# Eight buffers for the last weights, GpSimd's norm written as an addition, scale products on ScalarE, and one operation for mask and maximum, in a two-layer gated kernel

## The chip, the core and the metric

The kernel runs on one core of a Trainium2 chip. The metric is the device time of one execution in microseconds. The engines are named as the profile names them: PE (TensorE, matmuls), PEld (its weight loads), DVE (VectorE), ACT (ScalarE), POOL (GpSimd), and SP (SyncE), which here issues nearly all DMAs.

## What is computed

Two layers on x of shape (8, 256, 512), each an "attention" and a feed-forward network, both added through a gate:

```python
x = x + tanh(g_xattn[0]) * conv_attention(ctx, ctx, layernorm(x), taps, D)   # stage "conv"
x = x + tanh(g_ffn[0])   * ffn_a(layernorm(x), w1, w2, w3)                   # stage A
x = x + tanh(g_xattn[1]) * cross_attention(layernorm(x), ctx, mask)          # stage C
x = x + tanh(g_ffn[1])   * ffn_b(layernorm(x), w1, w2, w3)                   # stage B

layernorm(x) = (x - mean) / sqrt(var + 1e-5)
conv_attention: per head of 8 rows, outer products k_i * v_j, a causal convolution of
                length 512 with the head's taps, plus D times the product, times q_i, summed over i
ffn_a: h = silu(xq @ W1) * (xq @ W2); hq @ W3, rows quantised to 127 levels, W to -1, 0, 1 times a mean
cross_attention: softmax(where(mask, q @ ctx.T / sqrt(512), -1e30)) @ ctx, zero where no row is valid
ffn_b: as ffn_a with silu, quantised in groups of 64, W = sign(W) * mean|W|, width 2048
```

## The kernel before

Everything is written by hand, engine by engine: each engine runs its own Python block in program order, and semaphores tie them together. Nothing is reordered, so an engine that waits holds back all that stands behind it in its block. All four stages cut x into 16 tiles of 128 rows by 512, and every stage is a software pipeline over these tiles.

**Conv** (tiles n = 0 to 15). POOL's `pairs` writes the outer products of the context in two operations, a wide one (128x1536, L485) and a narrow one (128x256, L488). PE convolves them in two halves (`conv_block`, L627) and transposes the normed x (L615) and the result (L622). DVE multiplies by q (`products`, L1069 to L1078) and folds (`fold_heads`, L1084); POOL finishes (`finish_heads`, L502, L505) and adds the result to x (`add_result`, L509). ACT copies and squares, and beside that sums and rounds the weights of stage A (`sum_weight`, `ternary`), placed by the tables `ABS_STEP` and `TERN_STEP`.

**A** (tiles t). Per tile PE computes three chunks of the up product (`a_chunk`, L690, 24 matmuls) and the down product of tile t-2 (L702, 11 matmuls). Around it: POOL's `a_norm` (`ln_root`, L282 and L285, then `ln_norm`, L290), DVE's `a_scale_x` (a maximum over 512 and three small operations, the last of them L1106), ACT's `a_round_x` (L894), POOL's `a_integers_x` (L521), SP's transposing DMA `turn_x`; ACT's silu (L905), DVE's `a_product` (L1119); DVE's `a_scale_h`, ACT's `a_round_h` (L910), POOL's `a_integers_h`, SP's `turn_hidden`. Stage B's weights are made ready in between: `load_b(j)` fetches chunk j of 24 (512 KB each), `sign_b(j)` on ACT takes its sign and the sum of its magnitudes (L915, L917). There are two raw buffers for the chunks, so `load_b(j)` waits for `sign_b(j-2)`. x goes out to `x_between` (`store_between`) and comes back re-tiled (`reload`); stage C's normalisation starts with `c_stats`.

**C** (tiles i). PE: `scores` (L724), `turn_p` (L735), `c_turn_x` (L713), `readout` (L746), and the last two down products of A. DVE: `masked` (scaled score plus mask offset, L1150, then the negated maximum of a row, L1153), `weight`, `c_residual`, `c_stats(i+3)`, `b_stats`. ACT: `copy_p`, `c_copy_x` (L926), `softmax` (L933), and a `sign_b` in each tile from i = 3. POOL: `c_norm` and the first `b_norm`s.

**B** (tiles n). Per tile PE computes four chunks (`b_chunk`, L763, 16 matmuls each) and the down product of tile n-2 (`b_down`, L780, 32 matmuls), the last four of these in one piece at the end. A chunk m needs the pair of PSUM banks that DVE's product (`fb_product`, L1218) of chunk m-3 has read. The x of the next tile is scaled, rounded and split by `fb_scale_x`, `fb_deq_x` and `fb_low_x` on DVE and `fb_round_x` and `fb_high_x` on ACT, and transposed by SP's DMA `fb_turn_x`.

## Time and profile before

| | us |
|---|---|
| median of 3 runs | 732.58 (731.56 to 732.95) |
| the profiled execution | 732.03 |
| its span, first to last instruction | 730.2 |
| PE, busy | 693.4 (95%) |
| DVE, busy | 607.0 (83%) |
| ACT, busy | 372.4 (51%) |
| POOL, busy | 326.7 (45%) |
| stage conv on PE | 8.8 to 188.1 |
| stage A on PE | 188.1 to 306.0 |
| stage C on PE | 306.0 to 384.2 |
| stage B on PE | 384.2 to 725.6 |

A profile is one execution. "Busy" is the time in which an engine works on an instruction; the rest is waiting. A row of the waits says which engine's instruction waited, and for whose; a row of the windows gives for a stretch the busy time of each engine, the number of its instructions, and the TensorE clock that was granted as a share of 2.4 GHz. Durations of neighbouring instructions overlap a little, so sums of them are slightly above the time that they take.

### The profile page before, as it was taken

How to read it: one execution, taken by the hardware profiler on the slowest of the kernel's cores; microseconds unless marked ns; L12 is line 12 of the kernel's file. 1: busy time of each engine (PE TensorE's matmuls, PEld its weight loads, DVE VectorE, ACT ScalarE, POOL GpSimd, SP SyncE). 2: the span in 40 equal slices, each digit the busy share in tenths (PEclk: the TensorE clock that was granted, in tenths of full speed). 3: DMA queues.
4: the chain of work that ended last, by engine and by line, in shares of the span. 5: the costliest groups of instructions: out<-in, count | busy, mean ns of one | idle time of the engine just before them, and what ended most of it. 6: DMA issues, size and time to landing. Idle time of an engine off the chain costs nothing.

```text
span 730.2 us, 9410 instructions
## 1 busy us (share of the span) xinstructions
PE 693.4 (95%) x3162; PEld 388.4 (53%) x3162; DVE 607.0 (83%) x1094; ACT 372.4 (51%) x541; POOL 326.7 (45%) x362
## 2 busy tenths in 40 slices
PE   5999999988889999899989999999999999999897
PEld 3777777766534444466664444444444444444343
DVE  3998888898899998756985899988888888898871
ACT  3255976281366668546887644443444334433430
POOL 5679788878787665467870002211011111110000
PEclk9999999999999999999999999999999999999999
DMA  8563363320046878979554433334223343332133
GB/s 281 195 242 127 107 247 129 116 78 10 7 113 163 161 166 171 206 252 389 169 145 116 101 73 88 84 76 83 56 63 75 86 88 88 72 87 65 37 73 101
DMA packets 140288, 90.97 MB, mean 125 GB/s; under 512 B 118992, under 2 KB 118992, under 8 KB 140240
## 3 DMA queue, kind: packets, MB, share of 16 engines
q1 hardware_dynamic: 138512, 86.35, 44.1%
q0 software_dynamic: 1200, 3.93, 1.6%
q8 instruction: 25, 0.41, 0.2%
q14 instruction: 23, 0.19, 0.1%
q10 hardware_dynamic: 528, 0.09, 0.1%
HBM read 53.04 MB, written 8.47 MB: 84 GB/s over the span
## 4 chain that ended last, share of the span: by engine, by line
PE 65%; DVE 18%; POOL 6%; DMA 4%; ACT 4%; issue 3%; SPq 0%; POOLq 0%; ACTq 0%; DVEq 0%
PE psum L763 26%; PE psum L627 18%; PE psum L780 14%; DVE phase_space L1119 3%; DVE a_scalars L1125 3%; POOL phase_space L290 3%; PE psum L724 2%; PE psum L746 2%; DVE ln_bn L276 2%; DVE a_scalars L1106 1%; DMA phase_space<-in_L_weights 1%; DVE a_scalars L1099 1%; DVE x_sb L1137 1%; DMA x_sb<-x_between 1%; PE psum L615 1%
## 5 line engine op out<-in xcount | busy, mean ns | idle before, releaser
L763 PE MATMUL psum<-phase_space 128*128 128x512 f16 x1024 | 225.3, 381 | 3.9 <-DMA phase_space<-phase_space 3.2
L627 PE MATMUL psum<-phase_space 128*128 128x288 f32 x640 | 165.3, 414 | 14.3 <-DVE phase_space L1258 8.8
L763 PEld LDWEIGHTS psum<-phase_space 128*128 128x128 f16 x1024 | 100.2, 98 | 127.4 <-issue 4.7
L627 PEld LDWEIGHTS psum<-phase_space 128*128 128x128 f32 x640 | 121.3, 194 | 47.2 <-issue 8.8
L602 POOL DMA_DIRECT2D out<-x_sb x15 | 9.5, 630 | 293.9 <-DVE x_sb L1251 293.9
L780 PE MATMUL psum<-phase_space 128*128 128x512 f16 x512 | 112.6, 379 | 0.0
L290 POOL TENSOR_SCALAR phase_space<-x_sb,ln_ag,ln_rs 128x512 f32<-128x512 f32 x48 | 101.2, 2108 | 9.1 <-POOL ln_rs L285 7.4
L690 PE MATMUL psum<-phase_space 128*128 128x512 bf16 (+1 forms) x384 | 79.2, 361 | 4.7 <-DVE phase_space L1119 4.3
L780 PEld LDWEIGHTS psum<-phase_space 128*128 128x128 f16 x512 | 50.1, 98 | 60.4
L1024 ACT ACTIVATE phase_space<-psum,b_scalars 128x512 f32<-128x512 f32 x64 | 43.2, 681 | 74.6 <-PE psum L763 74.2
L1030 ACT ACTIVATE phase_space<-phase_space,magic 128x1024 f32<-128x1024 f32 x32 | 36.5, 1148 | 84.8 <-DVE phase_space L1230 84.8
L1218 DVE SCALAR_TENSOR_TENSOR phase_space<-psum,b_scalars,phase_space 128x512 f32<-128x512 f32 x64 | 47.6, 747 | 27.1 <-ACT phase_space L1024 26.4
L690 PEld LDWEIGHTS psum<-phase_space 128*128 128x128 bf16 x384 | 37.1, 98 | 45.4 <-DVE phase_space L1119 4.4
L1069 DVE TENSOR_TENSOR phase_space<-psum,phase_space 128x1024 f32<-128x1024 f32 x32 | 39.1, 1222 | 16.8 <-PE psum L627 16.6
L485 POOL TENSOR_TENSOR phase_space<-phase_space 128x1536 f32<-128x1536 f32 x16 | 48.6, 3040 | 3.5 <-DMA phase_space<-in_context_heads 3.5
L1173 DVE TENSOR_REDUCE phase_space<-phase_space 128x8 f32<-128x512 f32 (+1 forms) x32 | 47.3, 1479 | 0.6
L276 DVE BATCH_NORM_STATS2 ln_bn<-x_sb 128x6 f32<-128x512 f32 x64 | 43.4, 679 | 3.0 <-DMA x_sb<-x_between 2.9
L702 PE MATMUL psum<-phase_space 128*128 128x512 bf16 x176 | 41.2, 383 | 1.8 <-DMA phase_space<-phase_space 1.8
L1243 DVE TENSOR_TENSOR phase_space<-phase_space 128x512 f16<-128x512 f32 x64 | 39.8, 684 | 0.0
L1237 DVE SCALAR_TENSOR_TENSOR phase_space<-phase_space 128x1024 f32<-128x1024 f32 x32 | 37.8, 1223 | 1.3
L285 POOL TENSOR_TENSOR ln_rs<-ln_ve,neg_half 128x1 f32<-128x1 f32 x64 | 36.2, 566 | 5.3
L282 POOL TENSOR_SCALAR ln_ve<-ln_ag 128x1 f32<-128x1 f32 x64 | 13.2, 206 | 56.3 <-DVE ln_ag L278 54.0
(110 smaller groups left out, 1013.3 us busy)
## 6 DMA issues: line engine op xcount, KB each, us to landing
phase_space<-in_L_weights SPq DMA_DIRECT2D x24, 512.0 KB, 4.6
phase_space<-in_L_weights SPq DMA_DIRECT2D x12, 704.0 KB, 7.0
phase_space<-kpad SPq DMA_DIRECT2D x14, 512.0 KB, 4.1
phase_space<-in_context_heads SPq DMA_DIRECT2D x16, 384.0 KB, 4.8
x_sb<-in_x_tiles SPq DMA_DIRECT2D x16, 256.0 KB, 4.6
phase_space<-in_context_turned SPq DMA_DIRECT2D x8, 512.0 KB, 6.2
x_between<-x_sb SPq DMA_DIRECT2D x16, 256.0 KB
x_sb<-x_between SPq DMA_DIRECT2D x16, 256.0 KB, 6.1
```

Of the source, the lines that this page charges most:

```text
L276: nc.vector.bn_stats(ln_bn[:, stage, n % 2, :], x_sb[:, n, :]).then_inc(s_ln[stage], 1)
L290: nc.gpsimd.tensor_scalar(dst, x_sb[:, n, :], ln_ag[:, stage, n, 0:1], ln_rs[:, stage, n:n + 1], ALU.subtract, ALU.mult).then_inc(s_done, 1)
L485: nc.gpsimd.tensor_tensor(at(kv_k, E, [[NP, rows], [E, 3], [1, E]]), at(cx_sb[k], 0, [[EX, rows], [0, 3], [1, E]]), at(cx_sb[k], 1, [[EX, ...
L627: last = nc.tensor.matmul(at(bank(4 * hh + lo), 0, [[64, B], [1, NP]]), toep[n % 2][:, hh, (lo - li) * P:(lo - li + 1) * P], kv[n % 2][:, ...
L690: last = nc.tensor.matmul(bank(UPA[c][part])[:, 0:w], fa_qT[t % 4][:, kk, :], a_wT[part][:, kk, c0:c0 + w], start=(kk == 0), stop=(kk == L ...
L702: last = nc.tensor.matmul(bank(6 + t % 2), fa_hT[t % 2][:, c, :], a_wT[2][:, c, :], start=(c == 0), stop=(c == JA - 1))
L763: last = nc.tensor.matmul(bank(2 * (m % 3) + w), fb_qT[n % 2][:, kk % 2, kk // 2, :], b_wT[w][:, kk // 2, c * 512:(c + 1) * 512], start=(k ...
L780: last = nc.tensor.matmul(bank(6 + k), fb_hT[k][:, part, c, :], b_wT[2][:, c, :], start=(c == 0 and part == 0), stop=(c == JB - 1 and part ...
L1024: nc.scalar.activation(fb_s[m % 2], bank(2 * (m % 3)), ACT.Silu, scale=fb_sm[:, n % 4, 2:3]).then_inc(g_si, 1)
L1173: nc.vector.tensor_reduce(gx[:, 0, :], grouped(src), AX.X, ALU.max, apply_absolute_value=True).then_inc(s_steps, 1)
L1218: nc.vector.scalar_tensor_tensor(fb_h[n % 2][:, c * 512:(c + 1) * 512], bank(2 * (m % 3) + 1), fb_sm[:, n % 4, 3:4], fb_s[m % 2], ALU.mult ...
L1243: nc.vector.tensor_tensor(fb_tp[n % 2][:, 1, g * 512:(g + 1) * 512], fb_t[n % 2][:, g * 512:(g + 1) * 512], fb_tp[n % 2][:, 0, g * 512:(g ...
```

## The change

In words, by place:

- **Small scale products.** DVE's fourth small operation of `a_scale_x` (128x2) and of `a_scale_h` (128x1) go to ACT, each behind its rounding. DVE does `a_scale_x` for two instead of three tiles of stage A within conv, and `a_stats` for three instead of four; the rest comes in stage A.
- **Norm.** `ln_norm` on POOL adds a negated mean where it subtracted the mean; for the stages after conv a new small operation on POOL makes the negated mean.
- **Order in conv.** POOL's `a_norm` comes one tile later and behind `pairs` of the next tile, and for t = 0 `finish_heads` of the last tile comes in A. The narrow product of `pairs(0)` goes to DVE; ACT squares before it issues the DMAs of the taps and of D; SP stores the taps later; `sum_weight(1, 2)` comes one tile sooner.
- **Weights of B.** Eight raw buffers instead of two. Five loads start in the last conv tiles, eight stand in A. ACT has a `sign_b` in each of the tiles t = 2 to 13 of A and 7 in C, where it had 6 in A and 13 in C.
- **SP in A and C.** `turn_hidden` stands ahead of `turn_x`, reloads start one tile sooner, and the queue of C is written anew. `c_stats` on DVE runs further ahead.
- **Scores.** Mask offset, scale and maximum become one operation that also gives the row's minimum of the negated scores; `softmax` takes it with scale -1. The mask offsets are made in four pieces, the valid rows in two.
- **End of B.** In tile 14 DVE prepares the x of tile 15 one product sooner, ahead of `b_residual(11)`.

```diff
-        b_in = [view(R_M + k * BCH, [BCH]) for k in range(2)]
+        b_in = [view(R_B + AW + k * BCH, [BCH]) for k in range(6)] + [view(R_M + k * BCH, [BCH]) for k in range(2)]
...
         def ln_root(pool, stage, n):
...
+            if stage > 0:
+                nc.gpsimd.tensor_scalar(ln_nm[:, stage, n:n + 1], ln_ag[:, stage, n, 0:1], -1.0, 1.0, ALU.mult, ALU.mult
+                                        ).then_inc(s_rs[stage], 1)
...
-            nc.gpsimd.tensor_scalar(dst, x_sb[:, n, :], ln_ag[:, stage, n, 0:1], ln_rs[:, stage, n:n + 1],
-                                    ALU.subtract, ALU.mult).then_inc(s_done, 1)
+            nc.gpsimd.tensor_scalar(dst, x_sb[:, n, :], ln_nm[:, stage, n:n + 1], ln_rs[:, stage, n:n + 1],
+                                    ALU.add, ALU.mult).then_inc(s_done, 1)
...
+        ABS_STEP[1, 2] = 4
+        B_HOME = (0, 1, 2, 3, 4, 5, 6, 7, 1, 2, 3, 4, 5, 6, 7, 3, 5, 6, 7, 5, 6, 7, 6, 7)
+        B_EARLY = {10: 0, 11: 1, 12: 2, 13: 3, 14: 4}
+        B_FFN = {1: 5, 3: 6, 5: 7, 7: 8, 8: 9, 10: 10, 11: 11, 12: 12}
+        ROWS_FFN = {0: 0, 2: 1, 4: 2, 6: 3, 9: 4, 13: 5}
+        RELOAD_FFN = {11: (0,), 12: (1,), 13: (2,), 14: (3, 4), 15: (5,)}
+        SIGN_STEP = {3: 12, 4: 13, 6: 14, 8: 15, 10: 16, 12: 17, 14: 18}
+        C_EARLY = {13: (0,), 14: (1, 2), 15: (3,)}
+        C_STEP = {0: (4,), 1: (5,), 2: (6,), 3: (7,), 5: (8,), 6: (9, 10), 7: (11, 12), 8: (13, 14), 9: (15,)}
...
 # SP, start
-                sp.wait_ge(s_dadd, 1)
-                sp.dma_start(kpad[:, :], kp_sb).then_inc(s_kpad, 16)
                 for n in range(NT):
...
+                    if n == 0:
+                        sp.wait_ge(s_dadd, 1)
+                        sp.dma_start(kpad[:, :], kp_sb).then_inc(s_kpad, 16)
...
 # POOL, conv
-                    if n >= NT - 4:
-                        a_norm(n + 4 - NT)
+                    if n >= NT - 3:
+                        a_norm(n + 3 - NT)
...
 # ACT
+                square(0)
                 act.dma_start(kp_sb, taps_in).then_inc(s_kin, 16)
...
+                    nc.scalar.activation(sm[:, t % 4, 3:5], a_mean[:, 0:2], ACT.Copy, scale=sm[:, t % 4, 1:2]
+                                         ).then_inc(f_us, 1)
...
+                    nc.scalar.activation(sm[:, t % 4, 8:9], a_down[:, :], ACT.Copy, scale=sm[:, t % 4, 6:7]
+                                         ).then_inc(f_ds, 1)
...
-                    if t % 2 == 1 and t >= 5:
-                        sign_b((t - 5) // 2)
+                    if 2 <= t < 2 + NBA:
+                        sign_b(t - 2)
...
 # DVE
-                    nc.vector.tensor_scalar(sm[:, k, 3:5], a_mean[:, 0:2], sm[:, k, 1:2], None, ALU.mult
-                                            ).then_inc(f_xs, 1)
...
-                    nc.vector.tensor_tensor(sm[:, k, 8:9], sm[:, k, 6:7], a_down[:, :], ALU.mult).then_inc(f_hs, 1)
...
-                    nc.vector.scalar_tensor_tensor(at_v[i % 4], bank(2 + i % 2)[:, 0:C], SC, at_neg[:, i % B, :],
-                                                   ALU.mult, ALU.add).then_inc(c_m, 1)
-                    dve.wait_ge(c_m, 2 * i + 1)
-                    nc.vector.tensor_reduce(asm[:, i % 4, 0:1], at_v[i % 4], AX.X, ALU.max, negate=True).then_inc(c_m, 1)
+                    nc.vector.tensor_tensor_reduce(at_v[i % 4], bank(2 + i % 2)[:, 0:C], at_neg[:, i % B, :], -SC, -NEG,
+                                                   ALU.add, ALU.min, asm[:, i % 4, 0:1]).then_inc(c_m, 1)
...
+                dve.wait_ge(s_cx[0], 16)
+                nc.vector.tensor_tensor(at(first_kv, 32, [[NP, LB * G * B], [1, 4]]),
+                                        at(cx_sb[0], 0, [[EX, LB * G * B], [1, 4]]),
+                                        at(cx_sb[0], 4, [[EX, LB * G * B], [1, 4]]), ALU.mult).then_inc(s_kv, 1)
...
-                    if 3 <= n < NT - 1:
+                    if n == NT - 2:
+                        fb_scale_x(n + 1)
+                        fb_up_scales(n + 1)
+                    elif 3 <= n < NT - 1:
                         b_residual(n - 3)
                     fb_product(n, 1)
+                    if n == NT - 2:
+                        fb_deq_x(n + 1)
+                        fb_low_x(n + 1)
+                        b_residual(n - 3)
```

The order on three engines, row by row as the built programs have it. First DVE at the end of conv, from the last fold of tile 15's first half on; `a_scalars` are the row scales of stage A. Before:

```order
L1084 TENSOR_TENSOR phase_space<-phase_space 128x32x16
L1099 TENSOR_REDUCE a_scalars<-phase_space 128x1
L1102 TENSOR_SCALAR a_scalars<-a_scalars 128x1
L1105 RECIPROCAL a_scalars<-a_scalars 128x1
L1106 TENSOR_SCALAR a_scalars<-a_mean,a_scalars 128x2
L1069 TENSOR_TENSOR phase_space<-psum,phase_space 128x32x32
L1071 TENSOR_TENSOR psum<-psum,phase_space 128x32x24
L1073 TENSOR_TENSOR phase_space<-psum,phase_space 128x32x8
L1078 TENSOR_TENSOR phase_space<-phase_space,psum 128x32x3x8
L276 BN_STATS ln_bn<-x_sb 128x6
L278 BN_AGGR ln_ag<-ln_bn 128x2
L1299 TENSOR_TENSOR a_down<-a_mean,gates 128x1
```

After:

```order
L1144 TENSOR_TENSOR phase_space<-phase_space 128x32x16
L1129 TENSOR_TENSOR phase_space<-psum,phase_space 128x32x32
L1131 TENSOR_TENSOR psum<-psum,phase_space 128x32x24
L1133 TENSOR_TENSOR phase_space<-psum,phase_space 128x32x8
L1138 TENSOR_TENSOR phase_space<-phase_space,psum 128x32x3x8
L1177 SCALAR_TENSOR_TENSOR phase_space<-psum,a_scalars,phase_space 128x512 x2
L1144 TENSOR_TENSOR phase_space<-phase_space 128x32x16
L1159 TENSOR_REDUCE a_scalars<-phase_space 128x1
L1162 TENSOR_SCALAR a_scalars<-a_scalars 128x1
L1165 RECIPROCAL a_scalars<-a_scalars 128x1
L1177 SCALAR_TENSOR_TENSOR phase_space<-psum,a_scalars,phase_space 128x384
L277 BN_STATS ln_bn<-x_sb 128x6
```

The four operations of `a_scale_x`, the statistics and `a_down` stood around the last products; now the products stand alone, and the scale of x (without its last operation) comes behind the first two products of stage A and the last fold.

Next ACT in stage A, one tile with and one without its share of stage B's weights before (rows L905 are silu, L910 and L894 the roundings, L915 and L917 the weights):

```order
L905 ACTIVATE phase_space<-psum,a_scalars 128x512
L910 ACTIVATE phase_space<-phase_space,magic,a_scalars 128x1408
L905 ACTIVATE phase_space<-psum,a_scalars 128x512
L894 ACTIVATE phase_space<-phase_space,magic,a_scalars 128x512
L905 ACTIVATE phase_space<-psum,a_scalars 128x384
L915 ACTIVATE phase_space<-phase_space 128x1024
L917 ACTIVATE phase_space,b_abs<-phase_space 128x1024
L905 ACTIVATE phase_space<-psum,a_scalars 128x512
```

After, one tile of A:

```order
L958 ACTIVATE phase_space<-psum,a_scalars 128x512
L963 ACTIVATE phase_space<-phase_space,magic,a_scalars 128x1408
L967 ACTIVATE a_scalars<-a_down,a_scalars 128x1
L958 ACTIVATE phase_space<-psum,a_scalars 128x512
L945 ACTIVATE phase_space<-phase_space,magic,a_scalars 128x512
L947 ACTIVATE a_scalars<-a_mean,a_scalars 128x2
L958 ACTIVATE phase_space<-psum,a_scalars 128x384
L973 ACTIVATE phase_space<-phase_space 128x1024
L975 ACTIVATE phase_space,b_abs<-phase_space 128x1024
L958 ACTIVATE phase_space<-psum,a_scalars 128x512
```

Each of the twelve tiles now has the pair L973, L975 and the two small products L967 and L947.

Last, DVE in tile 14 of stage B, from the tile's first product on (`x_sb<-psum` is `b_residual`, `128x8` the group scales of the next x). Before:

```order
L1218 SCALAR_TENSOR_TENSOR phase_space<-psum,b_scalars,phase_space 128x512
L1247 TENSOR_TENSOR b_scalars<-b_scalars,b_fac 128x1
L1251 SCALAR_TENSOR_TENSOR x_sb<-psum,b_scalars,x_sb 128x512
L1218 SCALAR_TENSOR_TENSOR phase_space<-psum,b_scalars,phase_space 128x512
L1173 TENSOR_REDUCE phase_space<-phase_space 128x8
L1176 TENSOR_SCALAR phase_space<-phase_space 128x8
L1178 RECIPROCAL phase_space<-phase_space 128x8
L1179 TENSOR_REDUCE b_scalars<-phase_space 128x1
L1181 TENSOR_SCALAR phase_space<-phase_space 128x8
L1183 RECIPROCAL b_scalars<-b_scalars 128x1
L1185 TENSOR_SCALAR phase_space<-phase_space,b_scalars 128x8
L1194 TENSOR_TENSOR phase_space<-phase_space 128x512
```

After:

```order
L1280 SCALAR_TENSOR_TENSOR phase_space<-psum,b_scalars,phase_space 128x512
L1235 TENSOR_REDUCE phase_space<-phase_space 128x8
L1238 TENSOR_SCALAR phase_space<-phase_space 128x8
L1240 RECIPROCAL phase_space<-phase_space 128x8
L1241 TENSOR_REDUCE b_scalars<-phase_space 128x1
L1243 TENSOR_SCALAR phase_space<-phase_space 128x8
L1245 RECIPROCAL b_scalars<-b_scalars 128x1
L1247 TENSOR_SCALAR phase_space<-phase_space,b_scalars 128x8
L1256 TENSOR_TENSOR phase_space<-phase_space 128x512
L1261 TENSOR_SCALAR b_scalars<-b_fac,b_scalars 128x2
L1280 SCALAR_TENSOR_TENSOR phase_space<-psum,b_scalars,phase_space 128x512
L1268 SCALAR_TENSOR_TENSOR phase_space<-phase_space 128x512
```

The scaling of the last x now follows the tile's first product, and the residual that stood there comes behind it.

## Rows read from the trace of the kernel before

**Rows 1.** Waits of PE: us in total, times, longest

```profile
PE psum L627 <- DVE phase_space L1258: 8.8, 1, 8.8
PE psum L690 <- DVE phase_space L1119: 4.3, 3, 1.7
PE psum L713 <- POOL phase_space L290: 4.2, 3, 2.1
PE psum L627 <- POOL phase_space L488: 4.0, 2, 2.1
...
PE psum L627 <- ACT phase_space L852: 1.5, 1, 1.5
```

**Rows 2.** Windows: length, busy time (instructions) of each engine, PE clock, DMA

```profile
161.80:218.90 57.10, 47.86 (x216) 29.05 (x216) 51.65 (x87) 23.14 (x31) 47.93 (x50) 0.97 0.20 50
218.90:295.10 76.20, 76.17 (x375) 36.37 (x373) 70.39 (x141) 51.32 (x66) 47.17 (x48) 1.00 0.80 166
306.00:384.20 78.20, 70.68 (x304) 47.14 (x303) 58.11 (x162) 54.64 (x110) 58.34 (x60) 0.98 0.73 236
...
679.70:697.90 18.20, 15.33 (x66) 6.72 (x66) 13.26 (x20) 7.10 (x10) 0.00 (x0) 0.91 0.07 15
...
176.20:183.10 6.90, 6.89 (x23) 5.13 (x24) 5.31 (x11) 0.81 (x1) 5.01 (x7) 0.75 0.09 20
309.30:316.00 6.70, 6.70 (x26) 4.18 (x25) 1.69 (x5) 3.93 (x5) 4.08 (x4) 0.75 0.62 165
```

**Rows 3.** Groups by form, POOL: busy us, mean ns | idle before

```profile
L290 POOL TENSOR_SCALAR phase_space<-x_sb,ln_ag,ln_rs 128x512 f32<-128x512 f32 x48 | 101.2, 2108 | 9.1 <-POOL ln_rs L285 7.4 <-DVE phase_space L1194 0.6 <-DVE phase_space L1173 0.5
...
L521 POOL TENSOR_SCALAR phase_space<-phase_space 128x512 bf16<-128x512 f32 x16 | 9.9, 619 | 1.4 <-ACT phase_space L894 0.2
...
L493 POOL TENSOR_SCALAR ln_off<-ln_ag,ln_rs 128x1 f32<-128x1 f32 x16 | 4.3, 267 | 1.7
...
L282 POOL TENSOR_SCALAR ln_ve<-ln_ag 128x1 f32<-128x1 f32 x64 | 13.2, 206 | 56.3 <-DVE ln_ag L278 54.0
```

**Rows 4.** Timeline, POOL and DVE late in conv: start us, us

```profile
172.28 2.75 POOL L485 TENSOR_TENSOR phase_space<-phase_space 128x1536 f32<-128x1536 f32 x1
172.53 3.05 DVE L1084 TENSOR_TENSOR phase_space<-phase_space 128x512 f32<-128x512 f32 x1
```

**Rows 5.** Groups by form, ACT: stage A's work and stage B's weights

```profile
L905 ACT ACTIVATE phase_space<-psum,a_scalars 128x512 f32<-128x512 f32 x32 | 21.6, 676 | 12.7 <-PE psum L690 12.7
...
L905 ACT ACTIVATE phase_space<-psum,a_scalars 128x384 f32<-128x384 f32 x16 | 9.0, 563 | 0.0
...
L910 ACT ACTIVATE phase_space<-phase_space,magic,a_scalars 128x1408 f32<-128x1408 f32 x16 | 25.0, 1560 | 19.0 <-DVE a_scalars L1131 19.0
...
L894 ACT ACTIVATE phase_space<-phase_space,magic,a_scalars 128x512 f32<-128x512 f32 x16 | 13.0, 812 | 20.6 <-DVE a_scalars L1105 20.6
...
L915 ACT ACTIVATE phase_space<-phase_space 128x1024 f16<-128x1024 f32 x24 | 25.1, 1046 | 3.9 <-DMA phase_space<-in_L_weights 3.9
...
L917 ACT ACTIVATE phase_space<-phase_space 128x1024 f32<-128x1024 f32 x24 | 25.4, 1057 | 0.8
...
L917 ACT ACTIVATION_READ_ACCUMULATOR phase_space<-phase_space 128x1 f32 x24 | 4.5, 186 | 0.0
```

**Rows 6.** Groups by form, DVE: a small product, the two mask operations

```profile
L1106 DVE TENSOR_SCALAR a_scalars<-a_mean,a_scalars 128x2 f32<-128x2 f32 x16 | 12.1, 758 | 0.0
...
L1150 DVE SCALAR_TENSOR_TENSOR phase_space<-psum,phase_space 128x256 f32<-128x256 f32 x16 | 6.7, 422 | 13.9 <-PE psum L724 10.9 <-issue 3.0
L1153 DVE TENSOR_REDUCE attention_scalars<-phase_space 128x1 f32<-128x256 f32 x16 | 6.7, 420 | 0.5
```

**Rows 7.** Timeline, PE: last up products, then four down products

```profile
682.59 15.31 PE L763 MATMUL psum<-phase_space 128*128 128x512 f16 x64 [2.87 <-DMA phase_space<-phase_space]
697.74 27.79 PE L780 MATMUL psum<-phase_space 128*128 128x512 f16 x128
```

**Rows 8.** Timeline, DVE: first two products of tile 15 in B

```profile
691.74 1.40 DVE L1218 SCALAR_TENSOR_TENSOR phase_space<-psum,b_scalars,phase_space 128x512 f32<-128x512 f32 x2
```

274 lines of the change are left out of this document (159 added, 115 removed).

## The prediction

> **What bounds the kernel now.** I read three views in this order. The busy times on the page first: PE works 95% of the span, so no engine's total matters as such, and only time in which PE waits, or runs at a lower clock, can be won. Second, PE's waits, with the engine that each was for [rows 1]: 8.8 us at the start behind DVE's first folds, 4.3 for DVE's products of stage A, 4.2 for POOL's norm, 4.0 for POOL's narrow product, 1.5 for a copy on ACT. Third, the windows, which say where these lie [rows 2]. From 161.8 to 218.9 us (end of conv, start of A) PE is busy 47.86 of 57.10 us. From 218.9 to 295.1, the rest of A, it is busy 76.17 of 76.20: nothing can be won, but something lost. In stage C it is busy 70.68 of 78.20, and behind the last wait of B 15.33 of 18.20.
>
> After some waits the granted clock is lower: 0.75 from 176.2 to 183.1 and 0.75 from 309.3 to 316.0 [rows 2], means of stretches in which part ran at the lower of the two levels, 1.2 GHz. A stretch of 6.9 us at 0.75 does what 5.2 us at full clock would: each costs about 1.7 us more than its wait. Where such a wait goes, this goes too.
>
> **Part by part.**
>
> *Norm on POOL.* The 512-wide norm takes 2108 ns, while the same kind of operation on 512 elements with constants and add-multiply takes 619 [rows 3]. The new form is add-multiply, but with operands from memory. A one-element operation with such operands takes 267 ns beside 206 without [rows 3], so they cost 61 ns at least. Bounds: 619 + 61 = 680 ns if the subtraction was slow, 2108 if the memory operands were. I take 680, since the only slow row is the only one that subtracts. The added small operation costs 206 ns [rows 3]. Per norm: 2108 - 680 - 206 = 1.2 us less, or 0.2 more.
>
> *End of conv, start of A* (term 1). PE waits twice here for POOL, 4.0 us in all, which had put a norm and two other steps ahead of the next tile's products; then three times for DVE, 4.3 us [rows 1]. The window has 9.24 us idle and 1.7 of low clock: 10.9 us. The norm now stands behind the products, one tile later. DVE loses from these tiles one statistics and one scale step, and the small product, which takes 758 ns on average for two elements [rows 6]; the ACT operation that takes its place lies where ACT idles. New waits: DVE's first scale now needs a norm made one tile later, and by my sum it comes with it, within 1 us of slack that POOL's speed decides. x of tile 2 is scaled only behind the last fold, so its rounding, POOL's integers and the transposing DMA end about 1 us after PE is ready for it; the first hidden transpose about 0.4 us. Term: 10.9 - 1.4 = 9.5, of which I keep 9.0 for collisions of the next kind.
>
> A DVE fold ran 3.05 us, as long as POOL's wide product beside it (2.75 us), which had begun 0.25 us earlier [rows 4]; it waited for the end of it. The Trainium skill, "GPSIMD Engine Reference", section "Key points", says that GpSimd shares its SBUF interfaces with VectorE, in contention with DVE instructions in a two-port mode or with two SBUF inputs; the trace agrees. It speaks against two pieces of this change: the narrow product of tile 0, now on DVE while POOL's wide one starts, and folds near POOL's shifted products.
>
> *Start* (term 2). PE waited for the fold, which needs the taps; POOL's two products were done just before it, so that taking one from POOL gains nothing by itself. The new DVE product lies ahead of the folds. If it starts before POOL's wide one, it is hidden under the taps' DMA; if behind, DVE is held about 2.75 us [rows 4] and the folds start some 0.9 us late. The taps' second copy and D are now issued after the squares, and DVE waits for them between the first two statistics; behind it are queued the second fold, two statistics, POOL's roots and its next wide product. By the order, PE needs these only at tile 1, a conv tile away. Term: 0, from -0.3 to +0.9.
>
> *One Abs sooner* (term 3). The wait of 1.5 us for ACT's copy [rows 1] comes behind two Abs sums and four roundings. One sum moves to a tile in which ACT idles. Gain 1.4.
>
> *ACT in A.* Per tile: two silus of 676 and one of 563 ns, 1560 and 812 for the roundings, 1046 + 1057 + 186 for the weights [rows 5]: 6.6 us. The two small products have no row; bounds 0.1 (as much as lies beside others) and 0.2 each (as the 186 ns read). Total 6.8 to 7.0. PE's period is 76.20 us for 375 matmuls of 35 a tile [rows 2]: 7.11 us. So ACT fits, by a hair, in twelve tiles instead of six, and DVE loses 758 ns of its 70.39 / 10.7 = 6.6 us a tile [rows 2, 6]. Term 4: 0. SP's transposes now stand behind fewer waits, and DMA, busy 0.80 of this window [rows 2], carries some 2 MB more. At its end a late reload held DVE and gave PE waits of 1.3 us in all; reloads start earlier. Gain 1.0 (term 5).
>
> *Stage C* (term 6). Idle 7.5, low clock 1.7: 9.2 us. It starts with a wait for the norm of x 1; with POOL 1.2 us quicker and DVE no longer late it goes, and the low clock with it. Then PE waits for ACT's copies, which stand behind weights that the DMA brings late, 3.9 us of ACT idle [rows 5]. With eight buffers and 7 instead of 13 weight steps (2.3 us each) both causes go. The last waits are for POOL, then saturated with norms. New: `c_stats` two at a time in tiles 6 to 8, beside the group scales of B's first x in 8 and 9, which makes DVE about 3 us late for some 2.9 of slack; the first readout needs a load that is issued only when A's products are over; the copies before the first scores. I leave 1.2 us for these. The fused mask operation replaces 422 + 420 ns [rows 6]; it has no row. Below: 422, as either half. Above, nothing in the trace forbids several times that; DVE has (78.2 - 58.1) / 16 = 1.3 us a tile to spare [rows 2], so up to about 2 us it costs little. I take 0.5. Term: 9.2 - 1.2 = 8.0.
>
> *End of B* (term 7). The wait of 2.87 us for the last x goes, and 15.31 us for 64 matmuls should be 13.8, by the 27.79 us for the next 128: 4.4 us in sight [rows 7]. But it isn't all there. PE would start tile 15 at 679.7, and its fourth chunk, 10.4 us later, needs the banks of its first, whose product DVE does at 691.74 [rows 8], as before: behind tile 14's hidden scales, which nothing moves. It ends at 692.5, the fourth chunk at 695.9 instead of 697.9. A new wait of 2.4 us for DVE takes the place of 2.9 for a DMA; gain 2.0, and 0.9 of that may go to a low clock behind this wait, as after the old one. Term 1.2, from 0.3 to 2.1.
>
> **The sum.** 9.0 + 0 + 1.4 + 0 + 1.0 + 8.0 + 1.2 = 20.6 us. Against the profiled execution's 732.03: 711.4; the median of the runs lies 0.55 above, so 712.0 would be its fellow. In my estimates of waits left over I rounded up in C and in term 1 by about 1 us together; I forecast 711.
>
> **Rivals.**
>
> *The norm is no quicker* (memory operands were slow). For: no row shows a large operation with them at speed. Against: the subtraction is in that row alone. Each norm then costs 0.2 more. Term 1 loses 3 (DVE's first two scales wait for it), term 5 loses 0.5, and in C the waits for POOL, 4.2 us [rows 1], mostly stay. 711 + 7.5 = 718.5.
>
> *POOL's lock takes DVE.* Two folds near the end of conv are held, each up to 2.75 us by a wide product [rows 4], where the slack is about 1 us, and the first product too. 711 + 2 x 1.7 + 0.5 = 715. The rule of the Trainium skill cited above would have it so.
>
> *ACT is late in A.* If gaps between its instructions add 0.5 us a tile, the period is 7.5: 12 x 0.4 = 5 us, 716.
>
> *All goes well.* Every leftover (1.4 + 0.5 + 1.2 + 0.9 us) vanishes, and A starts clean: 707.
>
> *Slower: the fused operation.* It is one instruction of a rare form. DVE's other work in C is 58.1 - 16 x 0.84 = 44.7 us, 2.8 a tile. If it takes X, C takes 16 x (2.8 + X) once this is above 70.2. The rest of the change is worth 12.6 without C, so the whole is slower than before when 16 x (2.8 + X) > 78.2 + 12.6, from X = 2.9 us; at 3.3 it is 739. Seven times either half: unlikely, but nothing measured excludes it.
>
> *It doesn't do what it says.* If DMA, not buffers, bounds the weights in C, they come late still: DMA is busy 0.73 there [rows 2]; but 7 of the chunks and two context rows leave C. I give it no case of its own; it is within 715.
>
> **Chances.** Forecast (708.5 to 713.5) 0.50; all goes well 0.12; norm 0.14; lock 0.12; ACT 0.08; slower 0.04. A measurement can tell about 0.2% (1.5 us) from no change. Faster by more 0.94, within 0.02, slower 0.04. The range reaches from 705.5, below the case of all going well, to 719, above that of the norm, and leaves out the slow case and mishaps in pairs.
>
> **What would show it.** The norm's row near 0.7 us. No wait of PE for POOL's products, the conv's end 5 to 6 us sooner; a wait of about 1 us for a DMA at tile 2 of A; then 7.1 us a tile. Stage C near 70 us. No wait for the last x, a wait of about 2.4 us for DVE's product before the last chunk. The fused row under 1 us. Wrong would be: a norm at 2.1 us, a tile of A above 7.2 us, C above 73, or PE starting after 9.5 us.

## The result and the profile after

| | before | after |
|---|---|---|
| median of the runs, us | 732.07 (730.57 to 732.95, 4 runs) | 711.54 (710.20 to 713.35, 4 runs) |
| profiled execution: time, span | 732.03, 730.2 | 713.35, 711.6 |

The ratio of the runs is 0.9723, with a 95% interval from 0.9692 to 0.9754. That is 20.5 us by the medians; I had forecast 711.0. The profiled execution of the changed kernel was the longest of its four, so the two traces differ by 18.6 us only; where part of the rest may lie is told further down, at the end of stage B.

PE's waits in the changed kernel, in the view that answers to [rows 1]. Columns: who waited for whom; us in total, times, longest.

```profile
PE psum L678 <- DVE phase_space L1320: 8.7, 1, 8.7
PE psum L814 <- DVE phase_space L1280: 3.0, 2, 2.4
PE psum L797 <- issue: 1.1, 1, 1.1
PE psum L775 <- ACT phase_space L984: 0.9, 1, 0.9
PE psum L753 <- DMA phase_space<-phase_space: 0.8, 1, 0.8
PE psum L741 <- DVE phase_space L1177: 0.5, 1, 0.5
PE psum L786 <- ACT phase_space L991: 0.4, 1, 0.4
PE psum L673 <- DVE phase_space L1138: 0.4, 1, 0.4
...
```

No wait for POOL is left, neither for its products nor for its norm. The three rows left out are of 0.2 to 0.3 us. The wait at the start is the old one. New are 2.4 us before the last up chunk of stage B (in the second line) and 1.1 us for a context row in stage C.

The windows that answer to [rows 2]: end of conv with start of stage A, the rest of A, stage C, the last tile's up products in B, and the end of that. Columns: length; busy time (instructions) of PE, PEld, DVE, ACT, POOL; PE clock, DMA share, GB/s.

```profile
154.57:207.85 53.28, 51.98 (x244) 32.40 (x242) 49.05 (x81) 30.51 (x44) 40.88 (x55) 1.00 0.33 95
207.85:294.33 86.48, 85.70 (x421) 41.05 (x420) 78.16 (x145) 73.92 (x116) 45.69 (x76) 1.00 0.87 192
294.33:365.55 71.22, 68.34 (x303) 46.72 (x302) 50.73 (x160) 43.74 (x92) 34.59 (x78) 1.00 0.62 200
660.93:679.07 18.14, 15.77 (x66) 6.63 (x66) 13.20 (x19) 7.09 (x10) 0.00 (x0) 0.91 0.02 7
671.55:679.07 7.52, 5.15 (x17) 2.01 (x18) 3.72 (x6) 2.26 (x4) 0.00 (x0) 0.77 0.00 1
```

PE now idles 1.3 us where it idled 9.2, and 2.9 us in stage C for 7.5. Only the end of B is as long as before: 18.14 us here, 18.20 in [rows 2].

To compare many kernels I cut each span at the same six matmuls on PE: its first; the first up product of stage A; the first up product of A's tile 4; the first transpose of stage C; the first up product of B; the first of the last 128 down products. These are starts of rows in PE's timeline, and differences of them; all in us.

| kernel | first matmul | to A | to A, tile 4 | to C | to B | to last down | to end | span |
|---|---|---|---|---|---|---|---|---|
| before | 8.79 | 179.36 | 30.73 | 87.13 | 78.16 | 313.57 | 32.46 | 730.2 |
| changed | 8.66 | 173.45 | 25.74 | 86.48 | 71.22 | 313.52 | 32.53 | 711.6 |
| changed_again | 8.38 | 174.27 | 25.50 | 85.53 | 71.04 | 313.34 | 32.54 | 710.6 |
| tail_old_order | 8.52 | 173.60 | 25.51 | 86.49 | 70.81 | 312.25 | 32.52 | 709.7 |
| tail_early_product | 8.29 | 174.47 | 25.50 | 86.54 | 71.19 | 309.29 | 32.52 | 707.8 |
| norm_subtracts | 8.68 | 175.53 | 26.67 | 85.53 | 75.97 | 311.85 | 32.47 | 716.7 |
| before_norm_adds | 8.70 | 178.08 | 28.59 | 87.65 | 73.55 | 312.23 | 32.50 | 721.3 |
| mask_two_steps | 8.50 | 174.24 | 25.51 | 85.53 | 70.99 | 313.52 | 32.51 | 710.8 |
| small_products_dve | 8.58 | 173.08 | 26.69 | 87.94 | 71.44 | 311.85 | 32.52 | 712.1 |
| norm_earlier | 8.54 | 175.79 | 25.52 | 85.53 | 70.48 | 313.52 | 32.52 | 711.9 |
| norm_forms | 8.55 | 173.40 | 25.70 | 86.50 | 70.28 | 311.82 | 32.55 | 708.8 |
| two_buffers | 8.84 | 173.60 | 25.74 | 85.53 | 80.46 | 313.51 | 32.52 | 720.2 |
| start_as_before | 8.77 | 172.90 | 25.70 | 86.10 | 70.90 | 311.82 | 32.51 | 708.7 |
| three_repairs | 8.50 | 173.63 | 25.70 | 86.50 | 68.77 | 309.26 | 32.54 | 704.9 |

Three columns vary by themselves, without an edit near them. "To A" lies between 172.9 and 174.5 in the kernels with the new order and the quick norm, and with it goes what PE's first 14 matmuls take, 5.3 to 6.6 us, where 20 of them take 5.0 later on. Their granted clock reads 1.00 in every trace, so the profile doesn't show what slows them. "To C" lies at 85.5 or 86.5 (86.1 in start_as_before): in some executions PE waits once, 0.8 us (0.4 there), for a transposing DMA at tile 5 of A. "To last down" holds a low clock of 1.5 to 1.7 us in some executions, of which more below (in two_buffers it is one at the start of B). I read no cause from such differences.

### The profile page after: what moved, and what is told of

Read it like the earlier page. It is cut to its first block, busy times and chain, and to the rows that moved or that the text cites. A ratio compares the mean times of both kernels' runs of the same rounds, so it can differ in the third digit from the quotient of the medians.

```text
span 711.6 us, 9462 instructions
## 1 busy us (share of the span) xinstructions
PE 689.8 (97%) x3162; PEld 387.1 (54%) x3162; DVE 589.9 (83%) x1064; ACT 377.8 (53%) x573; POOL 270.6 (38%) x412
## 4 chain that ended last, share of the span: by engine, by line
PE 77%; DVE 10%; ACT 4%; POOL 3%; DMA 3%; issue 3%; SPq 0%; ACTq 0%; POOLq 0%; DVEq 0%
PE psum L814 26%; PE psum L678 17%; PE psum L831 15%; PE psum L741 7%; PE psum L753 4%; PE psum L797 3%; PE psum L775 3%; DMA phase_space<-phase_space 1%; DVE phase_space L1235 1%; DMA phase_space<-in_ctx 1%; DVE ln_bn L277 1%; DMA phase_space<-in_taps 1%; DVE phase_space L1280 1%; PE psum L666 1%; POOL phase_space L528 1%
## 5 line engine op out<-in xcount | busy, mean ns | idle before, releaser
L678 PE MATMUL psum<-phase_space 128*128 128x288 f32 x640 | 163.6, 411 | 8.9 <-DVE phase_space L1320 8.7
L297 POOL TENSOR_SCALAR phase_space<-x_sb,ln_nm,ln_rs 128x512 f32<-128x512 f32 x48 | 38.2, 795 | 23.0 <-PE psum L764 8.9
L958 ACT ACTIVATE phase_space<-psum,a_scalars 128x512 f32<-128x512 f32 (+1 forms) x48 | 30.7, 640 | 16.1 <-PE psum L741 15.8
L1177 DVE SCALAR_TENSOR_TENSOR phase_space<-psum,a_scalars,phase_space 128x512 f32<-128x512 f32 (+1 forms) x48 | 33.4, 697 | 6.9 <-ACT phase_space L958 5.9
```

What stands on the lines that cost most here:

```text
L678: last = nc.tensor.matmul(at(bank(4 * hh + lo), 0, [[64, B], [1, NP]]), toep[n % 2][:, hh, (lo - li) * P:(lo - li + 1) * P], kv[n % 2][:, ...
```

## Experiments

### What the norm's form is worth: norm_subtracts, before_norm_adds

The first puts the old form back into the changed kernel:

```diff
-nc.gpsimd.tensor_scalar(ln_nm[...], ln_ag[... 0:1], -1.0, 1.0, ALU.mult, ALU.mult)
-nc.gpsimd.tensor_scalar(dst, x_sb[:, n, :], ln_nm[...], ln_rs[...], ALU.add, ALU.mult)
+nc.gpsimd.tensor_scalar(dst, x_sb[:, n, :], ln_ag[... 0:1], ln_rs[...], ALU.subtract, ALU.mult)
```

> The changed kernel with POOL's norm in its old form, x minus mean times root, without the added small operation. The output is the same. Theory of the prediction (subtraction makes the norm slow, and the norm's speed is worth 7.5 us in the new order): the norm's row goes back from 0.8 to 2.1 us, and the kernel takes about 7.5 us more, near 719: about 3 at the start of stage A, 0.5 at its end, 4 in stage C, where PE waits for POOL's norms again. Rival (the gain came from the order and the buffers): the norm at 2.1 us is hidden behind other work, 0 to 2 us more.

Measured: 719.04 us (718.67 to 719.62, 6 runs), beside 710.85 for the changed kernel on the same chip; ratio to the kernel before 0.9835 (0.9809 to 0.986). The theory gave 719. The groups by form on POOL, first of this kernel (as in [rows 3]), then of the changed one: busy us, mean ns, idle before.

```profile
L294 POOL TENSOR_SCALAR phase_space<-x_sb,ln_ag,ln_rs 128x512 f32<-128x512 f32 x48 | 101.5, 2114 | 8.5 <-POOL ln_rs L289 7.5 <-PE psum L761 0.2 <-DVE b_scalars L1242 0.2
```

```profile
L297 POOL TENSOR_SCALAR phase_space<-x_sb,ln_nm,ln_rs 128x512 f32<-128x512 f32 x48 | 38.2, 795 | 23.0 <-PE psum L764 8.9 <-DVE phase_space L1256 6.8 <-POOL ln_rs L292 6.3
L289 POOL TENSOR_SCALAR ln_nm<-ln_ag 128x1 f32<-128x1 f32 x48 | 9.1, 190 | 3.8
```

With the slow norm PE waits for it again, five times in stage C (this is norm_subtracts; columns as in the first list):

```profile
PE psum L761 <- POOL phase_space L294: 5.1, 5, 2.0
```

By the stages: 4.9 us in C (75.97 for 71.04 in changed_again), 2.4 around the start of A (202.20 for 199.77, both columns together), nothing in the rest of A. In C a stretch at the lower clock stands behind the longest of these waits; the granted clock is 0.86 from 354 to 366 us.

The second does this part alone in the kernel before, with the same edit the other way round.

> The kernel before with one part of the change: POOL's norm as an addition, with the small operation that it needs (0.2 us); orders, buffers and all else as they were. In the changed kernel the norm's form was worth 8.2 us (719.0 without it, 710.9 with it). Theory A (each norm on the path counts, whatever stands around it): the waits for POOL's norm in stage C (4.2 us) and for its products late in conv (4.0) shrink by two thirds, with the low clocks behind them (3.4 us): 8 us less, near 724. Theory B (form and order need each other: the old order puts other work, late weights and late taps into the same gaps, so that a quick norm is followed by the next wait): 2 to 4 us less, near 729.

Measured: 725.83 us (723.09 to 726.82), ratio 0.9924 (0.9907 to 0.9941), 6.2 us by the medians: between the two theories, nearer to A. In stage C it brings 4.6 us (78.16 to 73.55), as much as it is worth in the changed kernel, and 3.4 around the start of A (210.09 to 206.67). But around the start of A PE's waits for POOL's products hardly shrank, from 4.0 [rows 1] to 3.3 us, and new ones came, as theory B says:

```profile
PE psum L633 <- POOL phase_space L494: 3.3, 2, 2.2
...
PE psum L696 <- DMA phase_space<-phase_space: 1.2, 1, 1.2
```

This trace is of the quickest of the six executions, 2.7 us below their median, and two stretches at the lower clock that the trace of before has aren't in it: from 176.3 to 183.2 us the granted clock is 1.00, behind a wait of 2.20 us for POOL, where it was 0.75 behind one of 1.88 [rows 2], and at the start of C, behind a wait of 0.98 us, it is 1.00 too. So about 1.7 of the 3.4 us around the start of A is clock and not waiting.

### Which form is slow: norm_forms

```diff
+nc.gpsimd.tensor_scalar(s, x, m, r, ALU.subtract, ALU.mult).then_inc(s_probe, 1)   # L596, in tiles 5 to 8 of B
+pool.wait_ge(s_probe, p + 1)
+nc.gpsimd.tensor_scalar(s, x, m, r, ALU.add, ALU.mult).then_inc(s_probe, 1)        # L598
...
```

> The changed kernel with eight added POOL operations after each of four residuals of stage B (tiles 5 to 8), where POOL idles; their results are used by nobody. All are tensor_scalar operations in fp32, in this order: 512 elements, subtract then multiply, operands from memory; add then multiply, memory; subtract then multiply, constants; add then multiply, constants; multiply then subtract, memory; multiply then add, memory; 256 elements, subtract then multiply, memory; add then multiply, memory. Theory A (the subtraction is slow, whatever its operands): 2.1, 0.8, 2.0, 0.62, 2.1, 0.8, then 1.05 to 1.1 and 0.4 us. Theory B (only the subtraction with operands from memory is slow): as A, but 0.62 for the third. Theory C (the old norm was slow through where it ran, in company with DVE, not through its form): all 512-wide ones between 0.6 and 0.8 us.

Its one run took 710.84 us. By the shortest times theory A holds for the six operations on 512 elements; those on 256 took about 0.15 us more than it says. The rows, on POOL by form, give means over four executions. L596 and L598 are subtract and add with operands from memory, L600 and L602 with constants, L604 and L606 multiply first and then subtract or add:

```profile
L604 POOL TENSOR_SCALAR phase_space<-x_sb,ln_rs,ln_ag 128x512 f32<-128x512 f32 x4 | 9.2, 2288 | 0.4
L596 POOL TENSOR_SCALAR phase_space<-x_sb,ln_ag,ln_rs 128x512 f32<-128x512 f32 x4 | 8.3, 2080 | 25.0 <-DVE x_sb L1338 25.0
L600 POOL TENSOR_SCALAR phase_space<-x_sb 128x512 f32<-128x512 f32 x4 | 7.7, 1923 | 0.3
...
L598 POOL TENSOR_SCALAR phase_space<-x_sb,ln_ag,ln_rs 128x512 f32<-128x512 f32 x4 | 4.1, 1029 | 0.4
L602 POOL TENSOR_SCALAR phase_space<-x_sb 128x512 f32<-128x512 f32 x4 | 3.9, 986 | 0.3
L606 POOL TENSOR_SCALAR phase_space<-x_sb,ln_rs,ln_ag 128x512 f32<-128x512 f32 x4 | 3.1, 768 | 0.4
```

The shortest are 2.08, 0.77, 1.92, 0.62, 2.08 and 0.77 us, and 1.23 and 0.55 for subtraction and addition over 256 elements. So a subtraction in either place of the operation costs 1.3 us more over 512 elements and 0.7 over 256, whatever its operands, and operands from memory cost 0.15 us. The two lengths give a price for each element, an estimate from the shortest times: (2.08 - 1.23) / 256 = 3.3 ns for the subtraction and (0.77 - 0.55) / 256 = 0.84 ns for the addition, beside 0.3 to 0.4 us that don't depend on the length. Why single additions took up to 1.3 us here (1.6 over 256 elements), and the kernel's own norms behind them up to 2.9, I didn't find out; each such norm stands in stage B, where nobody waits for it.

The Trainium skill, "GPSIMD Engine Reference", section "3.1 Elementwise — side-by-side cycle accounting", gives 768 ns for 512 elements as the best case of its loop, 1.8 cycles at 1.2 GHz for each, which is 1.5 ns. The addition with operands from memory took the same in all, 767 to 769 ns, but at 0.84 ns an element and a fixed part, so that the agreement of the totals is chance; the one with constants was quicker than that, 0.62 us. In both the measurement decides. The section doesn't speak of subtraction.

### Is it the order or the form: norm_earlier

```diff
-if n >= NT - 3: a_norm(n + 3 - NT)         # ahead of the next root
 if n + 3 < NT: ln_root(...); conv_offset(...)
 if n >= 2: add_result(n - 2)
+if NT - 4 <= n < NT - 1: a_norm(n + 4 - NT)
```

> The changed kernel with POOL's first three norms of stage A one tile earlier in conv and behind the residual addition, as in the kernel before; the norm's form stays the quick one. Theory (order counts with the quick norm as well): root and norm (1.8 us with the small operations) stand before the heads' sums again and may wait for DVE's statistics there, so the next tile's pairs come late and PE waits for them: 2 to 3 us more. Rival (only the slow norm made the order matter): within 0.5 us.

Measured: 713.90 us (713.52 to 715.09, 4 runs), ratio 0.9764 (0.9748 to 0.978), where the changed kernel has 0.972. PE's waits for POOL's products are back, though each norm is quick:

```profile
PE psum L678 <- POOL phase_space L534: 3.1, 2, 1.9
```

The way to tile 4 of A (both columns) is 201.31 us instead of 198.6 to 200.0 in the kernels with the new order and the quick norm. So order and form both count there, and neither alone brings the term. Over the same stretch before has 210.09, before_norm_adds (form alone) 206.67, norm_subtracts (the change without the form) 202.20, and the changed kernel 199.19 and 199.77: most of the term is the order and the work that moved with it.

### The small products: small_products_dve

```diff
-nc.scalar.activation(sm[3:5], a_mean[0:2], ACT.Copy, scale=sm[1:2]).then_inc(f_us, 1)
+nc.vector.tensor_scalar(sm[3:5], a_mean[0:2], sm[1:2], None, ALU.mult).then_inc(f_us, 1)
-nc.scalar.activation(sm[8:9], a_down, ACT.Copy, scale=sm[6:7]).then_inc(f_ds, 1)
+nc.vector.tensor_tensor(sm[8:9], sm[6:7], a_down, ALU.mult).then_inc(f_ds, 1)
```

> The changed kernel with both small scale products of stage A on DVE again (0.76 us and about 0.2), none on ACT (0.28 each). The output is the same. Theory: in the steady part of A neither engine bounds (DVE 6.4 of 7.13 us a tile, ACT 6.9), PE keeps its 7.13 us; at the start of A, where PE waits 0.5 us for DVE's product, DVE comes about 1 to 2 us later: 1 to 2 us more. Rival 1: nothing changes (within 0.3 us), the move was needed for nothing. Rival 2: ACT, relieved by 0.56 us a tile, ends waits elsewhere: a gain.

Measured: 714.01 us (713.85 to 714.69, 4 runs), ratio 0.9764 (0.9749 to 0.978). The theory had the start right and the place too small: the column to tile 4 is 1.0 us longer (26.69), but the rest of A, which I took for safe, is 87.94 us instead of 85.5 or 86.5, with waits of PE in mid-stage:

```profile
258.89 4.91 PE L741 MATMUL psum<-phase_space 128*128 128x512 bf16 x24 [0.22 <-DVE phase_space L1173]
279.77 2.32 PE L753 MATMUL psum<-phase_space 128*128 128x512 bf16 x10 [1.71 <-DMA phase_space<-phase_space]
```

The 6.4 us a tile of the expectation were the changed kernel's, without the two products. With them DVE has almost nothing left: from 228 to 278.62 us it is busy 49.17 of 50.62 us, where it is busy 46.67 of the same 50.62 in the changed kernel, and in the whole rest of A it waits for another engine once (1.4 us, for a reload). Its 1.21 us for a part of the valid rows, from 256.88, end just before the first of the two waits shown. The second is for a DMA; that it was late because DVE's scale of x stands ahead of it in the chain is read from the order and wasn't tried by itself.

### The mask in one operation: mask_two_steps

```diff
-nc.vector.tensor_tensor_reduce(at_v, scores, at_neg, -SC, -NEG, ALU.add, ALU.min, asm[0:1])
+nc.vector.scalar_tensor_tensor(at_v, scores, SC, at_neg, ALU.mult, ALU.add)
+nc.vector.tensor_reduce(asm[0:1], at_v, AX.X, ALU.max, negate=True)
```

> The changed kernel with the mask and the maximum of the scores as two operations again (422 and 420 ns in place of 505 for the one). The output is the same. Theory: DVE has time to spare in stage C, so 0.34 us more in each of 16 tiles shows only where PE waits behind DVE, at tiles 8 to 10 (0.4 and 0.9 us waits for ACT, which had waited for DVE): 0.3 to 1 us more. Rival (it is on the chain from scores to readout in each tile): 16 x 0.34 = 5.4 us more.

Measured: 713.04 us (711.50 to 714.60, 4 runs), ratio 0.975 (0.9731 to 0.9769), which overlaps with that of the changed kernel. Its trace shows no loss: stage C is 70.99 us, the span 710.8. One wait grew, for ACT behind DVE's maximum (1.15 us for 0.4 or 0.7); the one ahead of the fifth readout was smaller (0.2 us, for 1.1 and 0.4 in the two profiles of the changed kernel). The rival, 5.4 us, is out. By the medians this kernel is 2.2 us slower than changed_again and 1.5 slower than the first four executions, by the traces not at all; what the fused operation brings, from nothing to 2 us, stays open. Its rows in the changed kernel:

```profile
L1214 DVE CUSTOM_DVE_ANT_0 phase_space<-psum,phase_space 128x256 f32<-128x256 f32 x16 | 6.8, 422 | 13.8 <-PE psum L775 13.0 <-DVE valid L1389 0.7
...
L1214 DVE DVE_READ_ACCUMULATOR2_ANT attention_scalars<- 128x1 f32 x16 | 1.3, 83 | 0.0
```

### The buffers: two_buffers

```diff
-B_HOME = (0, 1, 2, 3, 4, 5, 6, 7, 1, 2, ...)      SIGN_STEP = {3: 12, 4: 13, 6: 14, ...}
+B_HOME = (6, 7) * 12                              SIGN_STEP = {i: i + 3 for i in range(3, 16)}
-if 2 <= t < 2 + NBA: sign_b(t - 2)
+if t % 2 == 1 and t >= 5: sign_b((t - 5) // 2)
```

The loads follow: none before stage A, six in it, the others where the changed kernel's row of loads has its own, the rest at its end.

> The changed kernel with two raw buffers for the last weights in place of eight, and so the old tables of their loads and signs: 6 chunks in stage A instead of 12, 13 in stage C instead of 7, each load behind the Abs sum of the chunk two before it. Norm, orders and fused operation stay new. Theory of the prediction (the buffers and the seven steps fewer were worth what PE waited for ACT's copies in stage C, 1.9 us, and part of the rest): 2 to 3 us more, in stage C alone, with waits of ACT for loads. Rival 1 (with the quick norm C has slack enough for 13 steps, 13 x 2.3 = 30 of 71 us of ACT's time): 0 to 0.5. Rival 2: stage A gains up to 0.8 us, since ACT and the DMA have less to do there, and it evens out.

Measured: 722.62 us (722.26 to 722.92, 4 runs), ratio 0.9867 (0.9853 to 0.9882): about 11 to 12 us more (start_as_before took 710.72 on the same chip), far outside what any theory gave. Stage A is as in the changed kernel, stage C takes 80.46 us instead of 71. ACT's and SP's waits in C (294 to 380 us):

```profile
ACT phase_space L972 <- DMA phase_space<-in_L_weights: 9.1, 3, 6.4
```

```profile
SPq L389 <- ACT phase_space L974: 41.6, 12, 5.2
```

SP stands 41.6 us at a load of a weight chunk, waiting for ACT's Abs sum of the chunk two before. The loads of weights behind it come late, and ACT then waits for them ahead of its copies. At the end of C, PE waits 3.5 us for the transposed first x of B. But this isn't the price of the buffers alone. The kernel before had two buffers as well, with a row of loads made for them, and took 73.55 us for stage C once its norm was quick. So against a fair opponent, the buffers, the fewer sign steps, SP's new queue, the statistics and the fused operation together are worth 73.55 - 71.1 = 2.4 us in C, less than the 3.8 that the prediction's 8.0 leaves for them beside its 4.2 for the norm; which of them brings it wasn't tried. What the experiment shows is that the changed kernel's row of loads can't be had without the buffers.

### The start: start_as_before

Tile 0's narrow product is back on POOL, behind the wide one.

```diff
-if n == 0: last.then_inc(s_kv, 1); return        # POOL, in pairs(n)
-nc.vector.tensor_tensor(...).then_inc(s_kv, 1)   # DVE, ahead of the first folds
```

> The changed kernel with the narrow product of tile 0 on POOL behind the wide one again, none on DVE. Prediction's theory (PE waits for DVE's folds, which need the taps' DMA, and POOL's products are done just before them): within 0.3 us, PE's first matmul at 8.4 to 8.9 us. Rival: the narrow product on POOL ends behind the folds: 0.5 to 1 us more.

Measured: 710.72 us (709.77 to 711.40, 4 runs), ratio 0.9705 (0.9688 to 0.9721); first matmul at 8.77 us. No difference from the changed kernel's 711.54 and 8.66, or from changed_again's 710.85 (on another chip), as both theory and term 2 said.

### The end of B: changed_again, tail_old_order, tail_early_product

> The changed kernel itself, as the yardstick for the runs beside it. In its first profile TensorE ran at a mean clock of 0.77 in the 7.5 us around its wait for DVE before the last up chunk, and 16 matmuls took 5.31 us for 3.45: 1.9 us. Theory: the low clock comes behind that wait in some executions and not in others, and is why its four times lie in two pairs (710.2 and 710.5, 712.6 and 713.4). Then this profile shows either 5.3 us and a span near 711.5, or 3.5 us and a span near 708.5 to 709.7. Rival: the low clock is there in every execution, and the spread is elsewhere. Ratio to the kernel before 0.970 to 0.974 either way.

Measured: 710.85 us (708.76 to 712.72, 6 runs), ratio 0.972 (0.9689 to 0.9751). Its profile has the low clock again, 16 matmuls in 5.13 us. But other kernels with the same end of B have it at full speed. The first row is the changed kernel's, the second norm_subtracts', which differs from it in POOL's norm alone:

```profile
673.92 5.31 PE L814 MATMUL psum<-phase_space 128*128 128x512 f16 x16 [2.37 <-DVE phase_space L1280]
```

```profile
680.77 3.63 PE L811 MATMUL psum<-phase_space 128*128 128x512 f16 x16 [2.37 <-DVE phase_space L1277]
```

Nine profiles have this order and this wait (all but before, before_norm_adds, tail_old_order and the two with the early product). The windows of 5 us behind the wait, first in the changed kernel, then in norm_subtracts:

```profile
673.92:678.92 5.00, 5.00 (x16) 1.97 (x17) 1.35 (x2) 0.69 (x1) 0.00 (x0) 0.66 0.00 0
```

```profile
680.77:685.77 5.00, 5.00 (x24) 2.29 (x25) 1.97 (x3) 1.37 (x2) 0.00 (x0) 1.00 0.00 0
```

The granted clock there is 0.66 to 0.69 in four of the nine (changed, changed_again, mask_two_steps, norm_earlier) and 1.00 in five, and in the 9.6 us ahead of the wait it is 1.00 in all. So the same wait is followed by a stretch at 1.2 GHz or isn't, and the column "to last down" falls into two groups, 313.3 to 313.5 and 311.8. The difference is 1.5 to 1.7 us. Both profiles of the changed kernel itself have the low clock, so that it comes and goes within one kernel is an inference: from the mean clocks of its other executions (0.996 to 1.00), and from kernels that differ only elsewhere. It is then part of what lies between its profiled execution and its median. I tried nothing that would tell what decides it.

```diff
-if n == NT - 2: fb_scale_x(n + 1); fb_up_scales(n + 1)          # and deq, low behind product 1
+if 2 <= n < NT - 1: fb_scale_x(n + 1); fb_up_scales(n + 1)      # behind product 1, deq and low behind product 2
```

> The changed kernel with the order of the last but one tile of stage B put back on DVE and ACT (scaling, dequantising and low part of the last x where they stood before). Theory of the prediction: the new order is worth 1.2 us, so this is 1.2 slower (0.3 to 2.1): the wait of 2.9 us for the last x's DMA is back in place of 2.4 for DVE's product. Theory after the first profile: the low clock behind either wait eats the difference; from the start of the last tile's up products (660.9 us there, 679.7 in the trace of before) to the down products it is 18.1 us with the new order and 18.0 with the old, so no difference that can be measured (within 0.5 us).

Measured: 713.21 us (711.68 to 714.89, 6 runs), ratio 0.9753 (0.9725 to 0.978). In its profile the old wait is back, and this time with the full clock behind it:

```profile
663.35 13.99 PE L814 MATMUL psum<-phase_space 128*128 128x512 f16 x64 [2.88 <-DMA phase_space<-phase_space]
```

So like must be set against like: to the last down products it takes 312.25 us (old order) or 311.8 (new) at full clock, 313.57 or 313.5 with the low one. The new order is worth 0.1 to 0.4 us in the traces. The medians differ by 2.4 us, with overlapping intervals, in the direction that the prediction's theory gave; how often each has the low clock would explain 1.5 at most, and the rest is open.

```diff
+if n == NT - 2: fb_silu(n + 1, 0)        # ACT, ahead of round_h
 scale_h(n)
+if n == NT - 2: fb_product(n + 1, 0)     # DVE, ahead of deq_h
```

> The changed kernel, with the silu of the last tile's first chunk on ACT ahead of the rounding of tile 14's hidden values, and DVE's product of it between tile 14's group scaling and its dequantising. Both work in time in which they wait now. Theory (DVE's late product is the bound): the wait of 2.4 us before the last up chunk goes, the low clock behind it (1.9 us) goes with it, and the last tile's up products take 13.8 us instead of 18.1: 4.3 us faster than the changed kernel, near 707. Rival 1: the wait comes back further on, for the hidden transposes of tiles 14 or 15, which now follow 0.75 us later behind tile 14: 0 to 2 us of gain. Rival 2: a low clock comes here without a wait: 2.4 us of gain alone.

Measured: 708.59 us (707.83 to 709.81, 6 runs), ratio 0.9692 (0.9665 to 0.9718). The wait is gone and its low clock too, and nothing came in its place. Its six times lie within 2.0 us where the changed kernel's spread over 4.0; but the six of norm_subtracts, which has the wait, lie within 1.0, so I don't put the spread down to it. PE's timeline from tile 14's first up product on, the first row 27.9 us for 128 matmuls without a gap:

```profile
647.55 27.89 PE L814 MATMUL psum<-phase_space 128*128 128x512 f16 x128
```

To the last down products it is 309.29 us, 4.1 less than changed_again and 2.5 less than those with the full clock. By the medians it is 2.3 us, 2 less than I expected, probably because the yardstick's median holds runs of both kinds.

### A kernel that beats both: three_repairs

Beside the early product, it takes up the two waits that the change left in stage C. SP's queue in the changed kernel: L377 reloads an x, L406 loads a context row; start us, us.

```profile
303.61 0.44 SPq L397 DMA_DIRECT2D phase_space<-in_context_turned  x1
304.09 0.44 SPq L391 DMA_DIRECT2D phase_space<-in_L_weights  x1
304.58 1.57 SPq L371 DMA_DIRECT2D x_between<-x_sb  x2
315.02 0.34 SPq L377 DMA_DIRECT2D x_sb<-x_between  x1
315.40 0.43 SPq L406 DMA_DIRECT2D phase_space<-in_ctx  x1
315.87 0.47 SPq L377 DMA_DIRECT2D x_sb<-x_between  x1
316.38 0.43 SPq L397 DMA_DIRECT2D phase_space<-in_context_turned  x1
316.86 0.43 SPq L377 DMA_DIRECT2D x_sb<-x_between  x1
317.33 0.43 SPq L406 DMA_DIRECT2D phase_space<-in_ctx  x1
```

SP stands about 9 us before the reload at 315.02, which needs the stores of 304.58 to have landed, and the rows of context 3 and 4 wait behind it without a reason of their own. Row 4 is issued at 317.33; loads of this kind take 7.4 us to land by the median, and PE's fifth readout, which needs it, starts at 325.26 after a wait of 1.1 us. The row of that wait names no engine, so that this reading rests on the order.

```diff
+load_memory(3); load_memory(4)
 reload(8)
-load_memory(3); ... load_memory(4)
-C_STEP = {..., 8: (13, 14), 9: (15,)}
+C_STEP = {..., 8: (13,), 9: (14,), 10: (15,)}
```

> The changed kernel with three repairs, each for a wait that its profile shows: the last tile's first product early (2.3 us by the median of that run alone), the loads of context rows 3 and 4 ahead of the reload that stands 9 us behind its store (PE waits 1.1 us for row 4 in one profile, 0.4 for ACT in another), and the statistics of stage C's last x in tiles 8, 9 and 10, one each, instead of two in tile 8 (PE waits 0.4 to 0.7 and 0.9 us for ACT, behind DVE's group scales of B's first x). Theory: 3.5 to 4.5 us less than the changed kernel, near 707. Rival: the waits in tiles 8 and 9 of stage C stay as they are, since the group scales alone (2.6 us) are longer than the slack: 2.5 to 3 us less, near 708.

Measured: 707.27 us (705.76 to 708.01, 4 runs), ratio 0.9655 (0.9641 to 0.967), beside 710.72 for start_as_before on the same chip, which is the changed kernel but for the start. Stage C takes 68.77 us, and one wait of PE is left in it:

```profile
346.81 1.99 PE L775 MATMUL psum<-phase_space 128*128 128x256 f32 x8 [0.45 <-ACT phase_space L984]
```

That answers the rival for stage C: the wait of tile 8 went, that of tile 9 halved. In all it is 3.4 us less than start_as_before, a hair under the 3.5 to 4.5 expected. The three repairs were tried together; of their shares only that of the early product was measured by itself (2.3 us).

## Why the prediction was right, and where its steps were off

Measured gains are from the table of stages, before against changed, in brackets before against changed_again. Terms 1 and 3 part at the start of conv's tile 14: 155.92 us before, 154.57 now.

| term | predicted | measured |
|---|---|---|
| 1, end of conv and start of A | 9.0 | 9.7 (with term 3: 10.3) |
| 2, start | 0 | 0.1 (0.4) |
| 3, one Abs sooner | 1.4 | 1.2 |
| 4 and 5, rest of A | 1.0 | 0.65 (1.6) |
| 6, stage C | 8.0 | 6.9 (7.1) |
| 7, end of B | 1.2 | 0.0 (0.2) |
| sum | 20.6 | 18.6 (19.6), 20.5 by the medians |

**Norm.** The step that carried most was right: the only slow row was the only one that subtracts. I had 680 ns, and it took 795 on average, 767 as a rule: operands from memory cost 0.15 us over 512 elements, not the 61 ns that I took from one-element rows. The rival "norm no quicker", priced at 718.5, was tried as norm_subtracts and gave 719.0, with the split that the prediction gives it (3 at the start of A, 0.5 at its end, 4 in C) measured as 2.4, 0 and 4.9.

**Term 1** came out 0.7 above the forecast; with term 3 it is 0.5 above in the first profile and 0.1 below in changed_again, whose first 14 matmuls took 0.7 us longer than those of before. Between the same two matmuls it was 62.96 us and is 53.28 now, with 1.3 us idle: 0.22 and 0.40 for DVE's products and 0.49 for its product in tile 2. The wait for a DMA of about 1 us at tile 2 didn't come; I had made x of tile 2 late by the order, and it was in time. One of 0.78 us came at tile 5 instead, and not in every execution.

**POOL's lock on DVE** was a rival, and here its mechanism is seen at work where the prediction hadn't looked, on a product of one element that the change moved from the end of conv to tile 12. First POOL's wide product, then DVE's operation, which has two inputs and ends with it; the fold in [rows 4] ended 0.55 us behind it, about as much as such a fold takes by itself:

```profile
153.40 2.75 POOL L528 TENSOR_TENSOR phase_space<-phase_space 128x1536 f32<-128x1536 f32 x1
153.62 2.54 DVE L1360 TENSOR_TENSOR a_down<-a_mean,gates 128x1 f32<-128x1 f32 x1
156.09 0.68 DVE L1144 TENSOR_TENSOR phase_space<-phase_space 128x512 f32<-128x512 f32 x1
```

It makes the fold behind it late; PE's next wait is 0.22 us for one of DVE's products, at 160.24, and whether it is for this I didn't try. The folds near the end of conv, on which the rival rested, ran 0.66 to 0.93 us: the last wide product (from 164.15 us) fell beside DVE's products with an input in PSUM, and these kept their 0.95 and 0.41 us. The rule of the Trainium skill that the prediction cites, two SBUF inputs, agrees with both. So the rival failed by phase, as far as one held operation shows, and not by mechanism.

**ACT in A.** The small products have rows now, which stand beside those of [rows 5]:

```profile
L947 ACT ACTIVATE a_scalars<-a_mean,a_scalars 128x2 f32<-128x2 f32 x16 | 4.5, 284 | 0.0
L967 ACT ACTIVATE a_scalars<-a_down,a_scalars 128x1 f32<-128x1 f32 x16 | 4.5, 281 | 0.0
```

They are above both of my bounds (0.1 and 0.2), and it changed nothing: A kept 7.13 us a tile. A price was to be had: the Trainium skill, "ScalarE: Activation LUTs", section "What ACT_TABLE_LOAD costs", gives 186 ns for an operation with constants, 93 more for each operand from memory and 0.83 an element; an estimate from these is 280 to 281 ns here, and the rows agree. Term 4, the move itself, I had at nothing because neither engine was full; small_products_dve shows that without it stage A loses 1.5 to 2.4 us. The step that failed there is to take a mean below the period for time to spare: I read DVE's 6.6 us a tile as slack, and with the small products and the rest of the change it is busy 97% of the stretch in which PE begins to wait. The move gained nothing against before, but the change couldn't have done without it.

**Stage C.** The leftovers were 2.8 us (2.3 in changed_again) instead of 1.2. I named their places partly: the statistics two at a time with group scales beside them (0.42 and 0.91 us), but not the wait for context row 4 (1.14 us, or 0.4 where ACT was the last). I had looked at what the first readout needs, not at the queue through which all rows pass, where a load that needs nothing stands behind a reload that waits 9 us. That is the rule of asking for each queue that a step is moved past, left out once. The fused operation took 422 + 83 = 505 ns, against 0.5 us taken.

**End of B.** The new wait was as predicted, 2.37 us for DVE's product before the last up chunk (2.4 forecast). The row that answers to [rows 8], behind tile 14's hidden values as there:

```profile
673.11 1.40 DVE L1280 SCALAR_TENSOR_TENSOR phase_space<-psum,b_scalars,phase_space 128x512 f32<-128x512 f32 x2
```

Its worth was mis-sized. I compared a row of before that held a low clock (15.31 us for 64 matmuls) with a new one at full clock and got 2.0 us, then took off 0.9 for a low clock that might come. Like for like it is 2.9 - 2.4 = 0.5 at most, and the traces show 0.1 to 0.4, while the medians of tail_old_order and changed_again differ by 2.4 and leave room for the whole term.

So part of the agreement is luck. Between the traces the sum was 2.0 us too large (term 1 too small by 0.7, terms 6 and 7 too large by 1.1 and 1.2), and it met the medians because the changed kernel's profiled execution was its longest.

## What to carry to other kernels

On GpSimd write x - m as x + (-m), and look out for a lone slow form in the list by form: here it was 1.3 us of 2.1 in each of 48 operations. Such a form counts wherever the operation stands on the path: with the old order the same edit gave 6.2 us by the medians, with the new one 8.2, each known to about 1.5, and by stages 4.6 and 4.9 in C, 3.4 and 2.4 around the start of A. So I don't call the two different. The order counts beside it: the changed kernel lost about 3 us once its quick norm stood ahead of the products again.

Go through an in-order queue entry by entry, and ask of each what it needs: a load that needs nothing must not stand behind one that waits. Before an engine is said to have time to spare, add up what the change itself puts on it, and look for its own waits: one that waits for nobody over a stretch is the bound there, whatever its mean. And before two stretches are compared, see at which clock each ran: the same wait of 2.4 us was followed by 1.5 to 1.7 us of low clock in four profiles and by none in five.

## What the runs showed of the hardware

- POOL, tensor_scalar on 512 fp32 elements: 2.08 us with a subtraction, 0.77 without, both with operands from memory; 1.92 and 0.62 with constants. At 256 elements 1.23 and 0.55, so 3.3 and 0.84 ns an element (estimates from the two lengths).
- A DVE operation on one element, two inputs in SBUF, took 2.54 us beside a wide two-input product on POOL, and operations with one input in PSUM weren't held by the same product.
- Behind the same wait of 2.4 us PE ran 16 matmuls in 3.6 us in five profiles and in 5.1 to 5.3 in four. Behind a wait of 1.88 us the granted clock was 0.75, behind one of 2.20 in another kernel 1.00.
- The fused scale, mask and minimum of 256 scores takes DVE 422 ns and 83 for the read of its result, as long as the plain operation that it contains.
